# Gated cross-attention block: the residual sum of batch 1 moves to GpSimd tile by tile, VectorE rounds all of x, and ScalarE splits unit 0's weights before batch 1's x is copied

## What is computed

```python
def quant(v, block):                    # per 1x128 of x, per 128x128 of ctx
    safe = maximum(amax(abs(block of v)), EPS)
    q = (v * (448 / safe)).astype(float8_e4m3fn)
    return q.astype(float32) * (safe / 448)

x = x + tanh(g_xattn) * einsum('emk,enk->emn', quant(layernorm(x)), quant(ctx_2048))
h = layernorm(x)
probs = softmax(h @ gate_w.T);  comb = top-4 of 8 experts, renormalised
moe = sum over e of comb[:, e] * ((silu(h @ wg[e].T) * (h @ wu[e].T)) @ wd[e].T)
sh  = silu(h @ swg.T) * (h @ swu.T) @ swd.T
x = x + tanh(g_ffn) * (moe + sigmoid(h @ shared_gate_w.T) * sh)
```

## Time and profile before

| | us |
|---|---|
| median of 3 runs | 174.49 |
| lowest, highest | 174.39, 174.8 |
| profiled execution, its own time | 174.46 |
| span in its profile | 172.7 |
| PE busy | 155.9 (90%) |
| DVE, ACT, POOL busy | 119.4, 102.5, 81.0 |

### The profile page before, as it was taken

One profiled execution on the slowest core, in us unless ns is written; L12 is line 12 of the kernel. 1 busy time (PEld: TensorE's weight loads), 2 busy tenths in 40 slices (PEclk: granted clock), 3 DMA queues, 4 the chain that ended last, 5 costly groups with the idle time before them and its releaser, 6 DMA issues.

```text
span 172.7 us, 2339 instructions
## 1 busy us (share of the span) xinstructions
PE 155.9 (90%) x707; PEld 124.7 (72%) x707; DVE 119.4 (69%) x252; ACT 102.5 (59%) x220; POOL 81.0 (47%) x104
## 2 busy tenths in 40 slices
PE   0038989999999999999999999999999999999991
PEld 0026448777888888877888888888888888888880
DVE  0988883897779688878989667933486655444553
ACT  2486953678669788565475545884654444555430
POOL 5340554246773675553356434453665544444410
PEclk9999999999999999999999999999999999999999
DMA  4499920000499994135223225205999100000003
GB/s 127 130 402 397 404 94 0 4 2 4 118 272 236 349 398 189 23 114 197 106 73 129 68 64 198 97 4 109 267 232 331 64 0 0 4 0 0 2 4 121
DMA packets 12913, 23.02 MB, mean 133 GB/s; under 512 B 3282, under 2 KB 4562, under 8 KB 12900
## 3 DMA queue, kind: packets, MB, share of 16 engines
q1 hardware_dynamic: 12180, 22.21, 40.5%
q10 hardware_dynamic: 720, 0.66, 1.2%
HBM read 21.51 MB, written 1.09 MB: 131 GB/s over the span
## 4 chain that ended last, share of the span: by engine, by line
PE 85%; DVE 5%; ACT 4%; DMA 2%; issue 1%; POOL 1%; DVEq 0%; POOLq 0%
PE bank L1158 52%; PE bank L1263 4%; PE bank L1265 4%; PE bank L1267 4%; PE bank L1271 4%; PE bank L1264 4%; PE bank L1270 4%; DMA x<-xs 2%; PE bank L1130 2%; PE bank L1113 1%; POOL x L357 1%; ACT cw L452 1%; ACT xc L460 1%; ACT cm L470 1%; DVE bn L707 1%
## 5 line engine op out<-in xcount | busy, mean ns | idle before, releaser
L362 POOL TENSOR_TENSOR w_lo<-w_raw,w_hi 128x512 fp32r<-128x512 f32 (+1 forms) x33 | 41.5, 1258 | 49.0 <-ACT w_hi L528 49.0
L1158 PE MATMUL bank<-h_hi,w_hi 128*128 128x512 f32 x130 | 51.5, 396 | 0.0
L1158 PE MATMUL bank<-h_hi,w_lo 128*128 128x512 f32 x130 | 50.7, 390 | 0.0
L1158 PE MATMUL bank<-h_lo,w_hi 128*128 128x512 f32 x130 | 50.7, 390 | 0.0
L549 ACT ACTIVATE a_hi<-bank 128x512 fp32r<-128x512 f32 (+1 forms) x34 | 20.3, 596 | 33.1 <-DVE bank L890 32.7
L375 POOL TENSOR_TENSOR w_lo<-w_raw,w_hi 128x256 fp32r<-128x256 f32 x33 | 24.4, 739 | 14.8 <-ACT w_hi L532 14.7
L899 DVE TENSOR_TENSOR a_lo<-bank,a_hi 128x512 fp32r<-128x512 f32 x32 | 22.0, 688 | 10.8 <-ACT a_hi L549 10.6
L890 DVE TENSOR_TENSOR bank<-silu,bank 128x512 f32<-128x512 f32 x32 | 22.2, 695 | 9.4 <-PE bank L1158 7.0
L1158 PEld LDWEIGHTS bank<-h_hi,w_hi 128*128 128x128 f32 x130 | 24.4, 188 | 5.4 <-POOL w_lo L362 0.3
L1158 PEld LDWEIGHTS bank<-h_hi,w_lo 128*128 128x128 f32 x130 | 24.4, 188 | 5.2
L1158 PEld LDWEIGHTS bank<-h_lo,w_hi 128*128 128x128 f32 x130 | 24.4, 188 | 4.8
(11 more groups left out here) (160 smaller groups left out, 215.8 us busy)
## 6 DMA issues: line engine op xcount, KB each, us to landing
w_raw<-w_full SPq DMA_DIRECT2D x32, 384.0 KB, 7.7
mix_b<-rows_dram SPq DMA_DIRECT2D x8, 256.0 KB, 6.6
mix_b<-rows_dram SPq DMA_DIRECT2D x4, 224.0 KB, 6.1
mix_b<-rows_dram SPq DMA_DIRECT2D x4, 192.0 KB, 5.9
out_t<-fin SPq DMA_DIRECT2D x3, 256.0 KB, 2.1
mix_b<-rows_dram SPq DMA_DIRECT2D x4, 160.0 KB, 6.0
x<-xs SPq DMA_DIRECT2D x2, 256.0 KB, 6.6
cw<-ctx_t SPq DMA_DIRECT2D x2, 256.0 KB, 7.0
```

What stands on the lines that cost most here:

```text
L362: nc.gpsimd.tensor_tensor(w_lo[:, n % 2, 0:cols], w_raw[:, n % RING, 0:cols], w_hi[:, n % 2, 0:cols].bitcast(F32), ALU.subtract).then_inc( ...
L1158: last = nc.tensor.matmul(out, w[k][a], x_of[k][b], start=(start and k == 0 and i == 0), stop=(stop and k == blocks - 1 and i == 2))
```

## The change

1. `sum_with_magic_x` and `transpose_less_sums` are gone with the constant `minus_eye`. Batch 0's x goes through `rounded` on DVE and `transpose_xq` on PE like batch 1's, and `copy_xqt(0)` reads a bf16 PSUM tile.
2. ACT calls `copy_xqt(0)` before `magic_ctx(1)`.
3. ACT makes the high parts of unit 0's gate and up weights (`high_first(0)`, `high_first(1)`, two instructions of 256 columns in place of one of 512) and of the router's weights before `copy_xqt(1)`, where they stood among and behind the two `residual0`.
4. The sums of `y2` and `x1` of both batches are made by POOL, each tile released by semaphores of its own tile. DVE's `residual_sum(1)` is gone.
5. POOL waits for `cq_ready[1]` and makes unit 0's gate low part ahead of these sums; `low_gate_w` goes behind the two `inverse_std1`.
6. `keep_clock_up(9)` becomes `keep_clock_up(6)`.

```diff
@@ gpsimd
-            def residual_sum_0():
-                pool.wait_ge(part0_done, 1)
-                pool.wait_ge(res0_ready, 1)
-                for j in tiles(0):
-                    nc.gpsimd.tensor_tensor(x1[:, j, :], x1[:, j, :], y2[:, j, :], ALU.add).then_inc(x1_ready[0], 1)
+            def residual_sum(b):
+                for jj, j in enumerate(tiles(b)):
+                    pool.wait_ge(part_done, j + 1)
+                    pool.wait_ge(res0_first, j + 1)
+                    nc.gpsimd.tensor_tensor(x1[:, j, :], x1[:, j, :], y2[:, j, :], ALU.add).then_inc(x1_ready[b], 1)
...
-                pool.wait_ge(gu_hi_done, 1)
+                if which == 0:
+                    pool.wait_ge(gate_hi_first, 1)
+                else:
+                    pool.wait_ge(gu_hi_done, 1)
...
-            residual_sum_0()
-            low_gate_w()
+            pool.wait_ge(cq_ready[1], 1)
             low_first(0)
+            residual_sum(0)
+            residual_sum(1)
             inverse_std1(0)
             inverse_std1(1)
+            low_gate_w()
             pool.wait_ge(y2_ready, 2)
@@ scalar
+            def high_first(which):
+
+                cols = slice(which * KC * P, (which + 1) * KC * P)
+                if which == 0:
+                    a.wait_ge(w_landed[0], 16)
+                nc.scalar.activation(w_hi[:, 0, cols], w_raw[:, 0, cols], ACT.Copy)\
+                    .then_inc(gate_hi_first if which == 0 else gu_hi_done, 1)
...
+            copy_xqt(0)
             magic_ctx(1)
-            copy_xqt(0)
+            high_first(0)
+            high_first(1)
+            high_gate_w()
             copy_xqt(1)
             residual0(0)
-            high_gate_w()
             residual0(1)
-            high_gu(0)
             high_d(0)
@@ vector
-            sum_with_magic_x(0, 1)
+            rounded(views_x(0), 1, xq_ready)
...
             residual1(0)
-            part_1 = residual1(1)
+            residual1(1)
             stats_x1(0)
-            residual_sum(1, part_1)
             stats_x1(1)
@@ tensor
-            transpose_less_sums(0)
+            transpose_xq(0)
             attend(0)
             transpose_xq(1)
             keep_clock_up(1)
             attend_by_tiles(1)
-            keep_clock_up(9)
+            keep_clock_up(6)
             transpose_x1(0)
```

More of the change, by code:

```diff
@@ L119, in flamingo_gated_block @@
         eye_b = sb("eye_b", [P, P], BF16)
-        minus_eye = sb("minus_eye", [P, P])
         bank = [stack.enter_context(nc.psum_tensor(f"bank{i}", [P, HN], F32)) for i in range(8)]
@@ L158, in flamingo_gated_block @@
         ctx_scaled = [sem(f"ctx_scaled{b}") for b in range(B)]
-        magic_done, clamped, x_summed = sem("magic_done"), sem("clamped"), sem("x_summed")
+        magic_done = sem("magic_done")
         cq_ready = [sem(f"cq_ready{b}") for b in range(B)]
@@ L172, in flamingo_gated_block @@
         y2_first = sem("y2_first")
-        part0_done = sem("part0_done")
+        part_done, res0_first = sem("part_done"), sem("res0_first")
         var1_ready, rstd1_ready = sem("var1_ready"), sem("rstd1_ready")
@@ L177, in flamingo_gated_block @@
         h_hi_done, h_lo_done = sem("h_hi_done"), sem("h_lo_done")
-        gate_lo_done = sem("gate_lo_done")
+        gate_hi_first, gate_lo_done = sem("gate_hi_first"), sem("gate_lo_done")
         gu_hi_done, gu_lo_done = sem("gu_hi_done"), sem("gu_lo_done")
@@ L259, in transpose_xq @@
             def transpose_xq(b):
-                sp.wait_ge(xq_ready, b)
+                sp.wait_ge(xq_ready, b + 1)
                 for jj, j in enumerate(tiles(b)):
@@ L317, in _ @@
                                     pattern=[[-1, E], [1, E]], channel_multiplier=0)
-            nc.gpsimd.tensor_copy(eye_b[:], eye[:])
-            nc.gpsimd.tensor_scalar(minus_eye[:], eye[:], -1.0, None, ALU.mult).then_inc(consts, 1)
+            nc.gpsimd.tensor_copy(eye_b[:], eye[:]).then_inc(consts, 1)
             def roots(b):
@@ L473, in copy_xqt @@
                 a.wait_ge(xqt_psum, b + 1)
-                src = QT[0][:].rearrange("p (k t) -> p k t", k=KC) if b == 0 else qt_view(b)
-                nc.scalar.activation(xqt[:, b], src, ACT.Copy).then_inc(xqt_ready, 1)
+                nc.scalar.activation(xqt[:, b], qt_view(b), ACT.Copy).then_inc(xqt_ready, 1)
             def residual0(b):
@@ L483, in residual0 @@
                         last = nc.scalar.activation(y2[:, j, ns], att_view(b, 0, jj)[:, ns], ACT.Copy, scale=deq[:, j, 0, n:n + 1])
-                last.then_inc(res0_ready, 1)
+                    if b < HB:
+                        last.then_inc(res0_first, 1)
+                if b >= HB:
+                    last.then_inc(res0_ready, 1)
             def copy_x1t(b):
@@ L748, in rounded @@
                 nc.vector.scalar_tensor_tensor(out, mag, LEAST * MAGIC, val, ALU.max, ALU.subtract).then_inc(done, 1)
[L750 to L757, removed]
             def scale_ctx1():
@@ L788, in residual1 @@
                                                               deq[:, j, 1, n:n + 1], x[:, j, ns], ALU.mult, ALU.add)
[L789 to L792, removed]
+                    if b < HB:
+                        last.then_inc(part_done, 1)
+                return did(last) if b >= HB else None
             def residual_sum(b, step):
                 after(step)
-                v.wait_ge(res0_ready, b + 1)
+                v.wait_ge(res0_ready, b - HB + 1)
                 nc.vector.tensor_tensor(x1[:, tile_slice(b), :], x1[:, tile_slice(b), :], y2[:, tile_slice(b), :], ALU.add)\
@@ L800, in stats_x1 @@
             def stats_x1(b):
-                if b == 0:
-                    for jj, j in enumerate(tiles(0)):
-                        v.wait_ge(x1_ready[0], jj + 1)
+                if b < HB:
+                    for jj, j in enumerate(tiles(b)):
+                        v.wait_ge(x1_ready[b], jj + 1)
                         step = did(nc.vector.bn_stats(bn[:, 1, j, :], x1[:, j, :]))
@@ L1081, in transpose_xq @@
             def transpose_xq(b):
-                pe.wait_ge(xq_ready, b)
+                pe.wait_ge(xq_ready, b + 1)
                 view = qt_view(b)
@@ L1086, in transpose_xq @@
                         last = nc.tensor.transpose(view[:, k, jj * P:(jj + 1) * P], xq[:, j, k, :], eye_b[:])
[L1087 to L1097, removed]
                 last.then_inc(xqt_psum, 1)
@@ L1133, in transpose_x1 @@
             def transpose_x1(b):
-                pe.wait_ge(x1_ready[b], BT if b == 0 else 1)
+                pe.wait_ge(x1_ready[b], BT if b < HB else 1)
                 transpose_tokens(b, x1, X1T, x1t_psum)
```

## The result

The changed kernel takes 173.25 us (median of 16 executions, 173.17 to 175.1) against 174.48 for the one before (16 executions, 174.39 to 176.22). The ratio over all executions (not the quotient of the medians) is 0.9936, 95% interval 0.9913 to 0.9959: a small gain, clear of the noise. The forecast was 173.1, range 172.75 to 174.1, faster. Ten of the 16 lie between 173.17 and 173.27, 1.1 to 1.2 us under the low end of before.

A forecast was written before the change was run, and what follows sets the result against it. PE's first product at 26.09 us, behind VectorE's queued sum of batch 1, was taken as the bound. Median 174.49 less 1.45 gives 173.04, plus 0.1 for a late clock rise: 173.1 us, range 172.75 to 174.1.

The forecast's parts named there:

- What bounds the kernel: From the first product at 26.09 us PE runs at its own pace, so a shift there moves the end equally.
- The rounding at no cost: VectorE, batch 0's x: rounding takes 0.43 us more, covered by idle time before 14.79, so it costs nothing.
- copy_xqt(0): ACT: batch 0's x copy goes ahead of magic_ctx(1), starting at 14.66 instead of 15.18 us.
- x of batch 1: PE and ACT: its copy starts at 16.91, not 17.32, so batch 1's product starts at 17.59, 0.38 us earlier.
- GpSimd's list: GpSimd: gate low part at 17.63, then four sums from 18.31 us, 0.68 apart, the last ending at 21.08.
- The variance of batch 1: VectorE: ready at 22.04 instead of 23.49, 1.45 us earlier: 0.68 its own sum, 0.77 batch 0's earlier sums.
- The powers: GpSimd, before normalising: each takes 0.79 or 1.08 us; 0.79 taken, gain 1.45, or 1.16 at the other end.
- PE's own queue: PE before the normalised tokens: six fillers leave 0.37 us of room; clock level rises at about 19.7.
- rule of 0.5 us for each us later than 20.4: PE's clock: each us by which the rise comes later costs PE 0.5 us; free up to 20.4.
- the first rival: PE's clock rises late, at 21.7 to 22.7 us, costing 0.65 to 1.15: 173.7 to 174.2 us; chance 18%.
- The rule on elementwise work: Adds belong on VectorE, GpSimd being about twice as slow: by it the moved sum would lose 0.7 us.
- The sum: Rounding nothing, batch 1's product -0.38 but hidden, its variance -1.45; 0.1 added for a late rise: 173.1 us.

The follow-up runs named there:

- the one with the epsilon on GpSimd: Changed kernel with 3, 2 and 1 fillers, batch 0's epsilon addition to the variance moved from VectorE to GpSimd behind its fourth sum: 173.5 us, ratio 0.9902.
- PE's list cleared: Changed kernel with 3, 2 and 1 fillers in place of 6, 4 and 2: 173.26 us, ratio 0.9916, first product at 7.99.
- sums by tiles on GpSimd without the early split: Kernel before with both batches' sums on GpSimd by tiles, low weight parts behind the powers, 3, 2 and 1 fillers: 173.95 us, ratio 0.9958.

## Why the prediction was right, point by point

**What bounds the kernel: right.** After the first product PE waits nowhere, and from first product to last PE takes 142.6 to 142.7 us before and after; the shift is carried to the end in all kernels but the one with the epsilon on GpSimd.

**The rounding at no cost, copy_xqt(0), x of batch 1: right.** VectorE's list was unmoved, the product of batch 1 came at 17.63 (forecast 17.59), and it waited for the context by then. Undoing the rounding costs 0.2 against the 7.99 with PE's list cleared, since ACT's new order leans on it.

**GpSimd's list: right to 0.07.** First sum 18.24 for 18.31, last ending 21.03 for 21.08.

**The variance of batch 1: a term mis-sized.** The step "VectorE takes batch 0's at 19.64 and 19.99 and ends its variance by 20.9" left out what GpSimd's sum does to VectorE's small instruction: 0.53 for 0.17. The variance came 1.25 earlier, not 1.45, and the run with the epsilon on GpSimd gives the missing 0.21 back. The small instruction is not slower, it waits. In the eleven traces in which it meets a GpSimd instruction of two operands and 256 columns it takes from 0.36 to 0.60 us and ends 0.02 to 0.03 us behind that instruction: here at 21.05, the last sum at 21.03. The price is what is left of GpSimd's instruction. The trace of before had it already, overlooked:

```profile
20.87 0.73 POOL L369 TENSOR_TENSOR w_lo<-w_raw,w_hi 128x256 fp32r<-128x256 f32 x1 [0.19 <-ACT w_hi L528]
```

```profile
21.27 0.36 DVE L810 TENSOR_SCALAR ve<-mv 128x2 f32<-128x2 f32 x1
```

The difference ends at 21.60, the small instruction at 21.63, where the prediction counts with 0.17. I had looked for contention in the other direction, GpSimd slowed by VectorE. The sums were not slowed (2.79 for four, against 1.41 for two before). The Trainium skill ("GPSIMD Engine Reference", Specifications) names such contention with VectorE instructions in a 2-port mode, and not only with two SBUF inputs. The rows agree in so far as what was held is a one-input instruction; in which mode it ran, no row shows.

**The powers: right,** 0.71 and 0.80, the lower bound. With VectorE's sum of batch 1 back beside it, batch 0's power took 1.09 in both runs, so this contention is real and left with that sum.

**PE's own queue: right in kind.** In both profiled executions of the changed kernel the level rose at 21.5, 1.8 us later than in the one of before, and PE's list delayed the first product by 0.31 and 0.19 against the 7.99 of the kernel with fewer fillers. The forecast's rule of 0.5 us for each us later than 20.4 gives 0.55; most of the difference is the 0.2 by which the tokens came later anyway. So the rise of the first rival came (21.5, where it had 21.7 to 22.7), at less than half its price of 0.65 to 1.15. That the level rises late because of the lost work was not shown.

**The rule on elementwise work.** The Trainium skill's advice ("GPSIMD Engine Reference", Engine selection) to keep such sums on VectorE would have cost 0.38 us here by the run with the sum back on VectorE, though the sum does take twice as long on GpSimd, as it says.

**The sum:** 1.45 less 0.20 for the hold is 1.25, and 174.48 - 1.25 = 173.23, beside a measured median of 173.25. That the two meet so closely is partly luck. The 1.25 is what the kernel with 3, 2 and 1 fillers shows at its first product (9.25 to 7.99). In both profiled executions of the changed kernel PE's list took part of it, 0.94 and 1.06 were left, and measured again the median was 173.55 for 174.58, 1.03 less. The forecast had set aside 0.1 for the late rise and nothing for the hold; it came within 0.15 because the late rise cost little in most of the executions first measured, which is inferred from their times alone.

**Where the gain sits,** by first products with PE's list cleared, 9.25 to 7.99: sums by tiles on GpSimd without the early split 0.58; everything but batch 1's sum on GpSimd 0.88 (9.25 to 8.37); that sum 0.38 more. These overlap and don't add up part by part.

## What to carry to other kernels

An add that takes twice as long on GpSimd can still pay when on VectorE it would stand in a queue: price the queue's order, not the operation. Then look at what GpSimd's two-operand work runs beside: in these runs one-input VectorE instructions on SBUF next to it waited until it had ended, 0.53 for 0.17 and 1.15 for 0.73. Look for such rows in the trace of before, where one instruction stands with two lengths, and put GpSimd's work next to VectorE's reads of PSUM, its statistics, or its pauses, which kept their lengths here. Fillers that keep the clock up belong to the list of the engine that waits; when a change pulls the awaited data forward, they can become the wait.

## What the runs showed of the hardware

VectorE's addition on two columns of fp32 in SBUF took 0.53 us beside a GpSimd sum of two operands and 0.17 with GpSimd at rest or on its power of two columns. In eleven traces it ended 0.02 to 0.03 us behind GpSimd's instruction, which was the sum in nine and a difference in two. Statistics (0.74 for two) and the scaled products from PSUM (2.15 for eight) beside the same sums kept their lengths.

PE's level rose at moments from 18.6 to 21.7 us in thirteen profiled executions, with the old rounding on PE or without it, and at 16.7 in the one with four more fillers ahead of batch 0's product; the page's granted clock, 0.996 to 1.0 as a mean, shows none of this, only the fillers' spacing does (0.43 and 0.22 us).

The last store of the output landed in 3.7 us in one profiled execution and in 2.1 in the thirteen others, which moved that execution's end by 1.6 us with no change on any engine.
